# Perceiver block on one core: the last pair's loop is ordered anew, with the expert stage's preparation moved into and ahead of it

## The chip, the cores and the metric

One core of a Trainium2 chip. The metric is the device time of one execution in microseconds (us), of which three runs are shown. TensorE does the matmuls, VectorE, ScalarE and GpSimd the elementwise work, SyncE issues the DMAs. All five run their own instruction streams and meet only at semaphores.

## The reference, cut to what matters

```python
x = x + xattn(ctx, layernorm(x), ...)      # 8 batches, 64 latents, 1024 context rows, 16 heads
x = x + mamba(layernorm(x), ...)           # 8 sequences of 64, 512 inner channels, 16 states
x = x + moe(layernorm(x), ...)             # 8 experts, gathered rows, gelu, weighted scatter-add

# mamba, for each of the 16 states n:
#   h = exp(dt * A[:, n]) * h + dt * x * B[:, n]      a scan over the 64 steps
#   y = y + h * C[:, n]
# then y = (y + x * D) * silu(z), and out = y @ W_out
# moe: h = gelu(rows[idx[e]] @ W1[e] + b1[e]); out[idx[e]] += (h @ W2[e] + b2[e]) * w[idx[e], e]
```

## The kernel before, in words

The 512 latent rows are four tiles of 128, each a pair of batches. Attention takes most of the time. The state scans of pairs 0 to 2 (48 units of one state each) run beside it. For one unit, GpSimd makes the drive (`open_unit`, line 630: dtx times a row of B), ScalarE the decays (line 1423), VectorE the scan (line 974), and GpSimd multiplies with a row of C (`times_c`, line 752); in the last units TensorE adds the products into a PSUM bank with an identity matmul (`sum_unit`, line 1967).

When attention ends, five units of pair 2 are left over (`left`), and pair 3, the last, has not begun: its rows exist only now. From here the kernel goes through these steps:

- The last pair's normalisation, input projection, convolution and time steps. VectorE writes the time steps `dts_l` (line 1194) and `dtx_l` (line 1197), between them the scans of left-overs 0 to 2 and the picks, the 0/1 matrices with which rows are gathered (`first_pick`, line 1033).
- The last pair's loop over 16 states. GpSimd makes drive n (line 777), with four drive buffers. ScalarE writes decays n into PSUM (line 1558). VectorE scans (line 1208) and multiplies with C (`read_open`, line 1218). TensorE adds the product into a bank (`sum_states`, line 2019). GpSimd does left-overs 3 and 4 ahead of drives 0 and 2, VectorE scans them in states 0 and 1, TensorE sums them in states 1 and 2. Pair 2 is gated by VectorE in state 6 (line 1230) and multiplied with W_out in state 8 (line 1808), and its rows are added and their statistics taken in state 11.
- Side jobs in the loop. TensorE turns one pick for each of the experts (line 2024), the coefficients (line 2039) and two products with b2 (line 2048), ScalarE evicts each from the one bank JB (lines 1540, 1543, 1546). Slot weights (line 2062, 4 matmuls for an expert) follow in states 12 to 15, two experts in each. Two of the gather matmuls (line 2054) stand in state 14 and two behind the loop.
- Behind the loop, GpSimd scales each tile's rows (`f_nat`, line 803), ScalarE rounds them (`f_hi`, line 1595), GpSimd subtracts (`f_lo`, line 806). TensorE gathers rows for the experts with 2 matmuls for each of 4 tiles, 2 groups of experts and 2 halves of the channels: 32 in all. The last tile's parts come from VectorE (lines 1250, 1253) and ScalarE.
- ScalarE evicts four banks of gathered rows (line 1577), loads the Gelu table (line 1582) and the experts follow: first products (line 2147), Gelu (line 1587), second products (line 2157), weighting (line 1266), scatter (line 2134).

Each engine's order is written out by hand, and a wait holds up all that is behind it on its engine. Reads of a work buffer wait for its sum (`v_acc`), reads of a product buffer for `sum_states` two states earlier (`m_acc`), and decays n for scan n - 2 (`m_scan`). The rows of B for states 4 to 15 are loaded (`b_all`, line 523) behind the load for left-over 4, which waits for the sum of left-over 0.

## Time and profile before

| | us |
|---|---|
| median of 3 runs | 768.75 |
| lowest, highest | 768.65, 770.01 |
| the profiled execution's own time | 769.03 |
| its span, first to last instruction | 767.3 |

The span is that of the profiled execution; 1.73 us lie around it. Below, PE is TensorE's matmuls, PEld its weight loads, DVE VectorE, ACT ScalarE, POOL GpSimd, SPq the DMA queue. A line of a timeline is one instruction or a run of equal ones (x2 and so on): its start and duration in us, and in brackets the idle time before it with the instruction that ended it. A duration holds the time for which the instruction was held up once it had begun. Consecutive instructions of an engine overlap by some hundredths of a microsecond. The loop goes from VectorE's first scan of line 1208 to the last product of line 1218.

### The profile page before, as it was taken

To read this page: it belongs to the slowest core of one execution; us is meant where nothing else is said; L and a number is where in the kernel's file an instruction comes from. 1 tells how busy PE (TensorE), PEld (TensorE's weight loads), DVE (VectorE), ACT (ScalarE), POOL (GpSimd) and SP (SyncE) were. 2 spreads that over 40 slices of the span, in tenths; PEclk is the share of its full clock that TensorE was granted. 3 is DMA by queue.
4 is the path that set the end of the run, shared out by engine and by line. 5 is a ranking of instruction groups with operands and counts; after the bars stand their busy time and mean duration, and the time that the engine had idled before them with its cause. 6 is when DMAs were issued, how large, how long until landed. Compare 5 with 4: busy or idle time off the path is not lost.

```text
span 767.3 us, 14591 instructions
## 1 busy us (share of the span) xinstructions
PE 735.2 (96%) x5539; PEld 681.3 (89%) x5539; DVE 493.9 (64%) x1061; ACT 432.5 (56%) x1135; POOL 399.7 (52%) x355
## 2 busy tenths in 40 slices
PE   8999999999999999999999999999999886999995
PEld 8889999999998999999989999999999663578885
DVE  7574574556574667858777778686798886840102
ACT  2546456546355766566578666666656553734331
POOL 6515315302610389658838986587397978730000
PEclk9999999999999999999999999999999995999999
DMA  8742100011001200310211022000100107703800
GB/s 308 243 138 60 63 25 2 1 62 25 2 5 59 53 16 1 95 34 16 65 32 34 15 68 55 15 15 1 33 15 21 28 22 234 254 1 129 285 26 30
DMA packets 51418, 49.62 MB, mean 65 GB/s; under 512 B 19524, under 2 KB 46352, under 8 KB 50320
## 3 DMA queue, kind: packets, MB, share of 16 engines
q1 hardware_dynamic: 51344, 48.64, 20.9%
q8 instruction: 46, 0.75, 0.4%
q14 instruction: 28, 0.23, 0.1%
HBM read 44.10 MB, written 4.52 MB: 63 GB/s over the span
## 4 chain that ended last, share of the span: by engine, by line
PE 69%; POOL 14%; issue 8%; DVE 5%; ACT 3%; DMA 1%; POOLq 0%; DVEq 0%
PE psum L1701 18%; PE psum L1736 17%; PE psum L1717 5%; PE psum L2157 4%; PE psum L2147 4%; POOL work L630 3%; PE psum L1670 3%; POOL work L637 2%; POOL y_sum L643 2%; PE psum L1767 2%; PE psum L1677 2%; PE psum L1795 2%; POOL drive L777 1%; PE psum L1611 1%; PE psum L1777 1%
## 5 line engine op out<-in xcount | busy, mean ns | idle before, releaser
L1347 ACT ACTIVATE pt_hi<-psum 128x512 fp32r<-128x512 f32 (+1 forms) x192 | 87.2, 489 | 179.9 <-PE psum L1717 122.0
L1736 PE MATMUL psum<-kvn_hi,pt_hi 128*128 128x256 f32 x512 | 150.1, 293 | 0.0
L1736 PE MATMUL psum<-kvn_hi,pt_lo 128*128 128x256 f32 x512 | 144.3, 282 | 0.0
L1736 PE MATMUL psum<-kvn_lo,pt_hi 128*128 128x256 f32 x512 | 144.2, 282 | 0.0
L1043 DVE TENSOR_REDUCE rowmax<-psum 128x1 f32<-128x728 f32 x64 | 58.6, 915 | 79.2 <-PE psum L1701 79.2
L1736 PEld LDWEIGHTS psum<-kvn_lo,pt_hi 128*128 128x128 f32 x512 | 97.4, 190 | 0.2
L1736 PEld LDWEIGHTS psum<-kvn_hi,pt_hi 128*128 128x128 f32 x512 | 97.1, 190 | 0.2
L1736 PEld LDWEIGHTS psum<-kvn_hi,pt_lo 128*128 128x128 f32 x512 | 97.1, 190 | 0.0
L1701 PE MATMUL psum<-kvt_hi,qk_hi 128*128 128x364 f32 (+1 forms) x384 | 90.5, 344 | 0.0
L896 DVE TENSOR_TENSOR pt_lo<-psum,pt_hi 128x512 fp32r<-128x512 f32 x128 | 82.0, 682 | 8.2 <-ACT pt_hi L1347 8.2
L637 POOL TENSOR_TENSOR work<-work,bc 128x512 f32<-128x512 f32 x40 | 54.3, 1357 | 58.6 <-DVE work L974 58.6
L1701 PE MATMUL psum<-kvt_hi,qk_lo 128*128 128x364 f32 (+1 forms) x384 | 84.5, 328 | 0.0
L1701 PE MATMUL psum<-kvt_lo,qk_hi 128*128 128x364 f32 (+1 forms) x384 | 84.5, 329 | 0.0
L974 DVE TENSOR_TENSOR_SCAN work<-dec,work 128x512 f32<-128x512 f32 x48 | 73.6, 1536 | 6.4 <-POOL work L630 6.1
L575 POOL TENSOR_SCALAR cvar<-cmv 128x8 f32<-128x8 f32 x8 | 1.9, 232 | 131.5 <-DVE cmv L835 131.1
L630 POOL TENSOR_TENSOR work<-dtx,bc 128x512 f32<-128x512 f32 x48 | 65.2, 1361 | 8.4 <-DMA bc<-dbc_keep 6.6
L1717 PE MATMUL psum<-ident,prob 128*128 128x128 f32 x512 | 66.5, 273 | 1.4 <-DVE pt_hi L893 0.8
L1701 PEld LDWEIGHTS psum<-kvt_lo,qk_hi 128*128 128x128 f32 x384 | 66.6, 188 | 0.0
L1701 PEld LDWEIGHTS psum<-kvt_hi,qk_lo 128*128 128x128 f32 x384 | 66.5, 188 | 0.0
L1701 PEld LDWEIGHTS psum<-kvt_hi,qk_hi 128*128 128x128 f32 x384 | 63.2, 189 | 2.2 <-issue 0.4
L1423 ACT ACTIVATE dec<-dts,a_neg 128x126 f32<-128x126 f32 x192 | 60.7, 394 | 5.9 <-DVE work L974 5.3
L1467 ACT ACTIVATE prob<-psum,nbias 128x728 f32<-128x728 f32 x64 | 55.7, 870 | 13.4 <-DVE nbias L1045 11.1
(251 smaller groups left out, 1576.5 us busy)
## 6 DMA issues: line engine op xcount, KB each, us to landing
w<-in_L_ffn_W_dram SPq DMA_DIRECT2D x16, 1024.0 KB, 8.2
ctx_nat<-in_ctx_dram SPq DMA_DIRECT2D x8, 1024.0 KB, 5.1
bc<-dbc_keep SPq DMA_DIRECT2D x48, 128.0 KB, 4.5
q_cur<-q_keep SPq DMA_DIRECT2D x14, 128.0 KB, 3.0
q_keep<-q_t SPq DMA_DIRECT2D x1, 1536.0 KB, 6.0
wq_sb<-in_L_xattn_Wq_dram SPq DMA_DIRECT2D x1, 1024.0 KB, 10.6
wk_nat<-in_L_xattn_Wkv_dram SPq DMA_DIRECT2D x1, 1024.0 KB, 12.7
wv<-in_L_xattn_Wkv_dram SPq DMA_DIRECT2D x1, 1024.0 KB, 14.7
```

The costliest lines, as they stand in the source:

```text
L630: pool.tensor_tensor(work[u % WORKS][:], dtx[:], bc[u % ROWS][:, 0:1, :].to_broadcast((P, DT, P)), ALU.mult).then_inc(v_drv, 1)
L637: link(pool.tensor_tensor(work[u % WORKS][:], work[u % WORKS][:], bc[u % ROWS][:, 1:2, :].to_broadcast((P, DT, P)), ALU.mult))
L896: dve.tensor_tensor(pt_lo[u][:, t0:t1, :], where.rearrange("p (t m) -> p t m", m=P), pt_hi[u][:, t0:t1, :].bitcast(F32), ALU.subtract).the ...
L974: dve.tensor_tensor_scan(work[u % WORKS][:].rearrange(flat), dec[u % 2][:].rearrange(flat), work[u % WORKS][:].rearrange(flat), 0.0, ALU.m ...
L1043: dve.tensor_reduce(rowmax[slot][:, hp, 0:1], LG_A, XY, ALU.max)
L1347: act.activation(pt_hi[u][:, t0:t1, :], where[:, 0:(t1 - t0) * P].rearrange("p (t m) -> p t m", m=P), ACT.Copy)\
L1423: last = act.activation(seqs(dec[u % 2][:])[:, d, :, 1:], seqs(dts[:])[:, d, :, 1:], ACT.Exp, scale=a_neg[:, d, n:n + 1])
L1467: act.activation(prob[hp % 2][:, 0:2 * CUT].rearrange("p (a n) -> p a n", n=CUT), LG_A, ACT.Exp, bias=nbias[slot][:, hp:hp + 1], scale=SCA ...
L1701: last = pe.matmul(psum[:, n, 0:x1_ - x0], w, x_[slot][:, k, x0:x1_], start=first, stop=final)
L1717: last = pe.transpose(TP[n][:, j * P:(j + 1) * P], prob[hp % 2][:, (4 * n + j) * P:(4 * n + j + 1) * P], ident[:])
L1736: pe.matmul(PV, w[u][:, j, :], x_[slot][:, j, :], start=(j == 0 and w is pt_hi and x_ is kvn_hi), stop=False)
L2147: last = pe.matmul(psum[:, f % 4, 0:P], w1[i][:, k, f * P:(f + 1) * P], xg_t[:, k, RING * q + i, :], start=(k == 0), stop=(k == CK - 1))
```

## The change

- GpSimd: behind the last attention left-overs it sets `fhalf`, takes the scales of tiles 0 and 1 in one go and makes all three parts of tile 0, then left-over 1's drive, tile 1's parts, left-over 2's drive. Drives 0 and 1 come ahead of left-over 1's product with C, and the rest of left-overs 1 to 4 is spread between drives 1 and 9. Tile 2's parts and tile 3's scale come behind drive 15.
- VectorE: left-overs 3 and 4 are scanned in states 2 and 4, the gate of pair 2 is in state 9, its addition and statistics in state 12, and the sum of the slot weights in state 10. Behind the loop it makes `f_hi` of the last tile itself, and evicts the second half of each gathered group.
- TensorE: left-overs 2, 3 and 4 are summed in states 1, 5 and 7, W_out of pair 2 is in state 9, the slot weights of one expert in each of the states 1 to 8, and eight gather matmuls (two tiles) in states 12 and 13. The second group gathers into banks 4 and 7.
- ScalarE: it no longer makes `f_hi`, loads the Gelu table ahead of the gathers' evictions, and evicts two banks of gathered rows instead of four.

The diff, cut to its core:

```diff
-        f_nat = [d[:].rearrange("p d m -> p (d m)")[:, h * C:(h + 1) * C] for d in dec for h in range(2)]
+        f_nat = [dec[0][:].rearrange("p d m -> p (d m)")[:, h * C:(h + 1) * C] for h in range(2)]
...
+        f_first = sb(open_, "f_first", [P, 2, C])
+        f_nat = [f_first[:, h, :] for h in range(2)] + f_nat
+        coef_slot = sb(open_, "coef_slot", [P, E])
...
-        GB = (0, 6)
+        GB = ((0, 1), (4, 7))
...
+        SUM_AT = {1: 2, 5: 3, 7: 4}
...
-            for u in left[1:3]:
-                open_unit(u)
+            link(pool.memset(fhalf[:], -0.5))
+
+            def row_scale(t0, t1):
+
+                pool.wait_ge(f_stat, t1)
+                link(pool.tensor_scalar(fvar[:, t0:t1], fmv[:, t0:t1, 1], 1.0, EPS, ALU.mult, ALU.add))
+                link(pool.tensor_tensor(frstd[:, t0:t1], fvar[:, t0:t1], fhalf[:, t0:t1], ALU.pow))
+
+            def row_parts(t):
+
+                pool.tensor_scalar(f_nat[t], x1[:, t, :], fmv[:, t, 0:1], frstd[:, t:t + 1], ALU.subtract,
+                                   ALU.mult).then_inc(f_ln, 1)
+                pool.wait_ge(f_ln, t + 1)
+                pool.tensor_scalar(f_hi[:, t, :], f_nat[t], 1.0, 0.0, ALU.mult, ALU.add).then_inc(f_hi_done, 1)
+                pool.wait_ge(f_hi_done, t + 1)
+                pool.tensor_tensor(f_lo[:, t, :], f_nat[t], f_hi[:, t, :].bitcast(F32), ALU.subtract)\
+                    .then_inc(f_lo_done, 1)
+
+            row_scale(0, 2)
+            row_parts(0)
+            open_unit(left[1])
+            row_parts(1)
+            open_unit(left[2])
...
-            times_c(left[1])
-            open_unit(left[3])
-            times_c(left[2])
-            open_unit(left[4])
             pool.wait_ge(v_dtx, INLINE + 1)
             pool.wait_ge(m_b, 2)
-            for n in range(2):
+            drive_open(0)
+            drive_open(1)
+            times_c(left[1])
+            drive_open(2)
+            open_unit(left[3])
+            drive_open(3)
+            times_c(left[2])
+            pool.wait_ge(ld_ball, 48)
+            drive_open(4)
+            open_unit(left[4])
+            drive_open(5)
+            drive_open(6)
+            times_c(left[3])
+            drive_open(7)
+            drive_open(8)
+            times_c(left[4])
+            for n in range(9, NS):
                 drive_open(n)
-            times_c(left[3])
-            for n in range(2, 4):
-                drive_open(n)
-            times_c(left[4])
-            pool.wait_ge(ld_ball, 48)
-            for n in range(4, NS):
-                drive_open(n)
-
...
+            row_scale(INLINE - 1, INLINE)
+            row_parts(INLINE - 1)
+            row_scale(INLINE, TT)
+            pool.sem_inc(f_rs, 1)
...
-                if n < 2:
-                    scan_unit(left[3 + n])
-                if n == NS - 10:
+                if n == NS - 7:
                     dve.wait_ge(v_acc, NS * INLINE)
                     dve.wait_ge(v_zc, INLINE)
                     gate = zs[(INLINE - 1) % 2]
                     dve.tensor_tensor(gate[:], gate[:], psum[:, WB, :].rearrange("p (d m) -> p d m", m=P), ALU.mult)\
                         .then_inc(v_y, 1)
-                if n == NS - 5:
+                if n == NS - 4:
                     mixed(INLINE - 1, psum[:, WB, 0:C])
                     out_stats(INLINE - 1)
                 if n >= 1:
                     read_open(n - 1)
+                if n in (2, 4):
+                    scan_unit(left[2 + n // 2])
+                if n == NS - 6:
+                    dve.wait_ge(f_cs, 1)
+                    dve.tensor_reduce(coef_slot[:], psum[:, 4, 0:2 * E].rearrange("p (e h) -> p e h", h=2), X, ALU.add)\
+                        .then_inc(f_cse, 1)
...
+            dve.tensor_scalar(f_hi[:, INLINE, :], x1[:, INLINE, :], fmv[:, INLINE, 0:1], frstd[:, INLINE:TT],
+                              ALU.subtract, ALU.mult).then_inc(f_hi_done, 1)
...
+                if isinstance(r, int):
+                    for g in range(EG):
+                        dve.wait_ge(f_gat, CK * (g + 1))
+                        dve.tensor_copy(xg_t[:, 1, g * RING:(g + 1) * RING, :],
+                                        psum[:, GB[g][1], :].rearrange("p (e s) -> p e s", s=P)).then_inc(f_gatd, 1)
...
-                    for k in range(CK):
+                    for k in range(1 if isinstance(r, int) else CK):
                         act.wait_ge(f_gat, CK * EG * r + CK * g + k + 1)
                         act.activation(xg_t[:, k, g * RING:(g + 1) * RING, :],
-                                       psum[:, GB[g] + k, :].rearrange("p (e s) -> p e s", s=P), ACT.Copy)\
+                                       psum[:, GB[g][k], :].rearrange("p (e s) -> p e s", s=P), ACT.Copy)\
                             .then_inc(f_gate, 1)
                 for q in range(EG):
...
+            act.activation(warm_out[:], a_neg[:, 0, 0:1], ACT.Gelu_apprx_tanh)
             longest = longest_list(act)
-            for t in range(TT):
-                act.wait_ge(f_ln, t + 1)
-                act.activation(f_hi[:, t, :], f_nat[t], ACT.Copy).then_inc(f_hi_done, 1)
...
             sum_unit(left[0])
+            spread_out(1)
             sum_unit(left[1])
-            spread_out(1)
-            sum_unit(left[2])
...
-                if n in (1, 2):
-                    sum_unit(left[2 + n])
                 sum_states(n)
-                if n == NS - 8:
+                if n in SUM_AT:
+                    sum_unit(left[SUM_AT[n]])
+                if n == NS - 7:
                     pe.wait_ge(v_y, INLINE)
                     w_out(zs[(INLINE - 1) % 2], psum[:, WB, 0:C]).then_inc(v_yo, 1)
                 if 1 <= n < E + 4:
                     side_job(n - 1)
-                weigh = n - E - 4
-                if weigh == 0:
+                if n == 1:
                     pe.wait_ge(f_hl, 1)
                     pe.wait_ge(m_b, 2)
-                if 0 <= weigh < E // 2:
-                    slot_weight(2 * weigh)
-                    last = slot_weight(2 * weigh + 1)
-                    if weigh == E // 2 - 1:
+                if 1 <= n <= E:
+                    last = slot_weight(n - 1)
+                    if n == E:
                         last.then_inc(f_cs, 1)
-                if n == NS - 2:
-                    pe.wait_ge(f_b2e, CK)
-                    pe.wait_ge(f_lo_done, 1)
-                    gather(1, 1, 0)
-            pe.wait_ge(f_b2e, CK)
-            pe.wait_ge(f_lo_done, 1)
-            gather(1, 0, 0)
+                t = n - E - 4
+                if t == 0:
+                    pe.wait_ge(f_b2e, CK + 1)
+                    pe.wait_ge(f_cse, 1)
+                if t in (0, 1):
+                    pe.wait_ge(f_lo_done, t + 1)
+                    for k in range(CK):
+                        gather(1, k, t)
...
-            for t in range(1, INLINE):
-                pe.wait_ge(f_lo_done, t + 1)
-                for k in range(CK):
-                    gather(1, k, t)
+            pe.wait_ge(f_lo_done, INLINE)
+            for k in range(CK):
+                gather(1, k, INLINE - 1)
```

## Rows read from the trace of the kernel before

**Rows 1.** The page: the span of the profiled execution.

```profile
span 767.3 us, 14591 instructions
```

**Rows 2.** Windows view: stretch; busy us (instructions) by engine; TensorE clock; DMA share, GB/s.

```profile
core 0: us, PE busy (x) PEld busy (x) DVE busy (x) ACT busy (x) POOL busy (x), PEclk, DMA share, GB/s
634.00:653.00 19.00, 13.70 (x27) 6.29 (x28) 12.92 (x13) 7.15 (x24) 16.50 (x13) 0.55 0.77 251
```

**Rows 3.** Chain of waits in order of time: start us, us, what, around the loop's end and the first expert.

```profile
678.56 0.79 PE psum L2062 x8
...
682.12 1.73 PE psum L1808 x8
683.85 5.14 PE psum L2054 x22
...
689.01 2.07 ACT xg_t L1577 x4
...
691.09 1.28 ACT L1582
...
695.41 3.72 PE psum L2157 x16
699.13 3.57 PE psum L2147 x32
```

**Rows 4.** Timeline of GpSimd: start us, us, line, operation, out<-in, count [idle before].

```profile
618.26 3.41 POOL L752 TENSOR_TENSOR work<-work,bc 128x512 f32<-128x512 f32 x2
622.98 1.27 POOL L630 TENSOR_TENSOR work<-dtx,bc 128x512 f32<-128x512 f32 x1 [1.30 <-PE psum L1967]
627.32 1.31 POOL L630 TENSOR_TENSOR work<-dtx,bc 128x512 f32<-128x512 f32 x1 [3.07 <-DMA bc<-dbc_keep]
...
639.19 2.48 POOL L777 TENSOR_TENSOR drive<-dtx_l,b_all 128x512 f32<-128x512 f32 x2
```

**Rows 5.** Timeline of GpSimd near the loop's end.

```profile
668.43 0.56 POOL L800 TENSOR_TENSOR frstd<-fvar,fhalf 128x1 f32<-128x1 f32 x1
669.21 1.23 POOL L803 TENSOR_SCALAR dec<-x,fmv,frstd 128x256 f32<-128x256 f32 x1 [0.22 <-POOL frstd L800]
675.96 0.73 POOL L806 TENSOR_TENSOR f_lo<-dec,f_hi 128x256 fp32r<-128x256 f32 x1 [5.52 <-ACT f_hi L1595]
```

**Rows 6.** Timeline of GpSimd near the kernel's start.

```profile
10.04 1.05 POOL L568 TENSOR_SCALAR x_hi<-x_lat 128x1024 fp32r<-128x1024 f32 x1 [1.97 <-DVE x_lat L854]
```

**Rows 7.** Timeline of VectorE ahead of the last pair's loop.

```profile
618.41 2.21 DVE L974 TENSOR_TENSOR_SCAN work<-dec,work 128x512 f32<-128x512 f32 x1 [0.89 <-POOL work L630]
...
633.27 2.29 DVE L1033 TENSOR_TENSOR pick<-iota_f,slot_of 128x1024 fp32r<-128x1024 f32 x1
640.56 1.22 DVE L1208 TENSOR_TENSOR_SCAN state<-psum,drive 128x512 f32<-128x512 f32 x1 [5.00 <-POOL drive L777]
```

**Rows 8.** Timeline of VectorE at the loop's end and after it.

```profile
676.71 1.26 DVE L1218 TENSOR_TENSOR read<-state,psum 128x512 f32<-128x512 f32 x2
...
683.89 0.42 DVE L1244 TENSOR_TENSOR x<-x,psum 128x256 f32<-128x256 f32 x1 [2.39 <-PE psum L1808]
...
686.00 0.41 DVE L1250 TENSOR_SCALAR dec<-x,fmv,frstd 128x256 f32<-128x256 f32 x1 [1.01 <-POOLq L801]
686.89 0.43 DVE L1253 TENSOR_TENSOR f_lo<-dec,f_hi 128x256 fp32r<-128x256 f32 x1 [0.49 <-ACT f_hi L1595]
```

**Rows 9.** Timeline of TensorE in and after the last pair's loop.

```profile
647.09 2.08 PE L2019 MATMUL psum<-read,ident 128*128 128x512 f32 x2 [4.76 <-DVE read L1218]
...
652.11 1.02 PE L1967 MATMUL psum<-work,ident 128*128 128x512 f32 x2
...
658.67 1.13 PE L2019 MATMUL psum<-read,ident 128*128 128x512 f32 x2 [0.32 <-DVE read L1218]
...
668.66 0.60 PE L2039 MATMUL psum<-ident,coef 128*8 128x128 f32 x4
...
679.75 1.02 PE L2019 MATMUL psum<-read,ident 128*128 128x512 f32 x2
```

**Rows 10.** Timeline of ScalarE in the loop.

```profile
669.66 0.57 ACT L1543 ACTIVATE coef_t<-psum 8x512 f32<-8x512 f32 x1
```

58 lines of the change are left out of this document (27 added, 31 removed).

## The prediction, made before the result was known

> **What bounds the kernel now.** I first read the page and the chain of waits for the whole span [rows 1], then timelines of each engine from 616 us on, since every edit lies there. The expert stage starts in earnest when TensorE begins the first expert's second products at 695.41 us; behind it TensorE hardly pauses [rows 3]. So the question is when that instruction starts. Three stretches lead to it.
>
> Ahead of the loop GpSimd is the late one. VectorE is done with its last pick at 635.56 and sits idle for 5.00 us until drive 0 is there; the loop's first scan starts at 640.56 [rows 7]. GpSimd was idle itself for 1.30 and 3.07 us earlier [rows 4]. In the loop the last product ends at 676.71 + 1.26 = 677.97, 37.4 us after the first scan [rows 8]. Behind the loop TensorE is the late one: it adds the last state only at 679.75 [rows 9], since slot weights and gathers stand in its queue, and then works off 22 gather matmuls in 5.14 us (0.234 each), after which ScalarE evicts for 2.07 us and loads a table for 1.28 [rows 3]. From the last product to 695.41 it takes 17.4 us.
>
> One mechanism matters throughout. A VectorE instruction whose two inputs lie in SBUF, and a GpSimd instruction, do not overlap. The scan at 618.41 took 2.21 us, the pick at 633.27 took 2.29, each held until GpSimd's instruction was over; the loop's scan, with one input in PSUM, took 1.22 beside GpSimd [rows 7]. GpSimd in turn took 3.41 us for two products that need 2.5 [rows 4].
>
> **Stretch 1, ahead of the loop.** GpSimd is free at 618.26 + 3.41 = 621.67 [rows 4]. From there it now has, up to the end of drive 0:
> - small operations for the scales: a memset and an addition (my estimate 0.4 with gaps) and a power of 0.56 [rows 5], a little more for two columns: 1.2 us together.
> - two times the rows' parts. `f_nat` 1.23, `f_lo` 0.73 [rows 5]. `f_hi` on GpSimd is not in this stretch. Its nearest row is a rounding with the same two constants, 1024 wide, 1.05 us [rows 6]; by width a quarter of it, with some fixed cost 0.4. The upper bound is `f_nat`'s 1.23, the same width but with two scalars read from memory. I take 0.4, as the operation is the same. With gaps, 2 x 2.6 = 5.2 us.
> - two left-over drives, one product with C, drive 0 at 1.24 [rows 4], `y_skip` (0.9) and the two small coefficient operations (0.5): 6.4 us.
>
> That is 12.8 us of its own work. Its two idle times are gone, so all of VectorE's two-input work now falls beside a busy GpSimd and holds it: two scans, two picks, `dts_l`, `dtx_l` and the latents' scaling, by the free durations about 1.0 + 1.0 + 1.0 + 1.1 + 0.65 + 0.7 + 0.3 = 5.75 us. Sum: 621.67 + 12.8 + 5.75 = 640.2. The first scan starts at 640.25, 0.3 us earlier. The four operations that leave this stretch (two products, two drives) are paid back by the rows' parts. With `f_hi` at 1.23 it would be 641.9.
>
> The Trainium skill, "GPSIMD Engine Reference", Engine selection, calls one-input work on GpSimd roughly line-rate and sends elementwise work to VectorE. By line rate the rounding of 256 columns would be an estimated 0.21 us and the sum 0.4 us less for two of them; by its advice the move is a loss. The trace has `f_nat` at 1.23 us on GpSimd [rows 5] and at 0.41 on VectorE [rows 8], which speaks for the advice and against line rate.
>
> **Stretch 2, the loop.** Up to state 5 GpSimd sets the pace: from drive 1 to drive 4 come six operations of 1.24, held by the third pick (1.1) and the scan of left-over 3 (1.1), so scan 4 can start 11.0 us into the loop. Then two scans and two products more (1.13 and 0.6 by their pitch), the scan of left-over 4 (1.1) and a wait of 0.7 for GpSimd ahead of it bring product 5 to 18.0 us, 658.3. Before, TensorE began to add state 5 at 658.67 [rows 9]: the same place, with both left-overs scanned in both.
>
> From there TensorE is the late one. Before, it went from state 5's sum at 658.67 to the coefficients' transpose at 668.66, that is 10.0 us for five sums of states, four turned picks, one spreading of C and W_out of pair 2 [rows 9], of which some 0.7 us were waits (0.32 ahead of the first). The change adds to the same stretch two sums of left-overs at 1.05 (1.02 by the row, and a gap [rows 9]) and four slot weights at 0.79 / 2 = 0.40 [rows 3]: 10.0 - 0.7 + 2.1 + 1.6 = 13.0. The transpose starts at 658.35 + 13.0 = 671.35. VectorE waits for it twice: at the gate of state 9 (for left-over 4's sum, 1.2 us) and at the new sum of the slot weights in state 10, behind which scan 11 is queued (1.1 us). ScalarE evicts the coefficients at 671.9 instead of 669.66 [rows 10], and behind that eviction stand decays 13, 14 and 15, each behind a side job. From the eviction to the last product it was 677.97 - 669.66 = 8.3 us and is 8.1 now. The last product ends at 680.0, **2.1 us later** than before.
>
> The loads of B are issued some 5 us later, as they hang on the sum of left-over 0; drive 4 is asked for at about 650, the loads should land at about 648. The experts' weights come 5 us later as well, and the first of them is not read before 686. Both I cost at nothing; if the first cover is gone, scan 4 waits by as much.
>
> **Stretch 3, behind the loop.** Counted from the last product: TensorE has only states 14 and 15 queued, so the last sum is done at +1.5 (before at +2.8, 679.75 + 1.02), VectorE's gate takes 0.7, W_out starts at +2.3 instead of +4.0, the row addition ends at +4.7 instead of +6.34 (683.89 + 0.42 [rows 8]). The last tile's `f_lo` ended 3.0 us after that addition (686.89 + 0.43 [rows 8]) and will again: one more VectorE operation of 0.4 in place of ScalarE's rounding: +7.7. TensorE has 4 + 12 gathers at 0.234 up to there, from +3.9: +7.65, in balance. So the last eight gathers start at +7.7 instead of at 688.34, that is +10.4: 2.7 us gained. From their start to xg ready it stays 1.9 us, as VectorE's copy (0.66 for 512 columns out of PSUM, half of 1.26 [rows 8]) is no faster than ScalarE's second (2.07 / 4 = 0.52 [rows 3]). But the table is loaded by then and ScalarE has two evictions less, so the first expert runs at TensorE's pace: 3.73 us for its first products, last Gelu 0.4: second products at +7.7 + 1.9 + 4.2 = +13.8 instead of +17.4. Gained: **3.6 us**. The experts' stage is unchanged.
>
> **Sum.** -0.3 is contained in the loop's end: +2.1 - 3.6 = -1.5 us. The profiled execution took 769.03 (span 767.3), 0.28 above the median of 768.75; its span would be 765.8 and its time 767.5, and against the median 767.2. A measurement of this kernel can tell about 0.2% (1.5 us) from no change, so this stands on that line.
>
> **The rivals.**
> - *The loop does not get longer (764.9).* If the sums and slot weights fit into TensorE's waits, the loop takes 37.7 us or less and -3.6 and -0.3 stand. For it: TensorE waited for products at 647.09 [rows 9], and is idle early in the loop. Against it: those waits are ahead of state 5, the added work is behind it.
> - *Drive 0 comes early (763.5).* Where GpSimd's `f_nat` and `f_hi` do not hold VectorE's scans and picks and dts_l is not late, the loop starts up to 3.5 us earlier. The rows show the hold for products alone. The Trainium skill, "SBUF — State Buffer", SBUF: two separate sides, says that any GpSimd operation holds the shared ports for its whole length; by that rule this rival falls.
> - *The gain is given back (768.7).* Each slot weight costs more than 0.40 alone, between other kinds of work, or `f_hi` costs 1.23 twice: the loop ends 1.5 us later still, and the time is the same.
> - *TensorE stays at the lower clock (772, slower).* In 634 to 653 us the granted clock was 0.55, near the lower level of 1.2 GHz; one sum of a state took 2.08 us at 647.09 and 1.02 for a pair of the same matmuls at 652.11 [rows 2, 9]. It rose after TensorE had worked without a pause from 647.09. The new order spreads TensorE's work there, with waits for products with C between. If the clock rises only at state 5, some 10 us of work up to there takes 20, the products wait, and the loop is about 5 us longer. It decides from the point where the clock is below 0.8 over the loop's first 16 us.
> - *The change does less than it says (767.9 to 768.7)*: the last tile's `f_lo` and not the gathers ends last behind the loop. This only moves the gain by a few tenths.
>
> **How the numbers follow.** My forecast (766.2 to 768.2) has 0.42, half of it below the line of 0.2%. The unchanged loop has 0.18, the early drive 0.08, the gain given back 0.12, the clock 0.10, and 0.10 are for a loop that is longer by 4 to 5 us by GpSimd's costs or late loads (769.5 to 771). Faster: 0.22 + 0.18 + 0.08 = 0.48. Same: 0.20 + 0.12 = 0.32. Slower: 0.20. The range runs from the early drive, 763.5, to 770.6, which leaves out the clock and a part of the last.
>
> **What would show it.** In the changed profile: first scan at 640.2 (early drive: 637); granted clock over the loop's first 16 us above 0.6; TensorE without waits between states 5 and 9 and the coefficients' transpose 13 us after state 5's sum; scan 11 waiting about 1 us for the slot weights; last product at 680.0; the first Gelu without a table load ahead and 13.8 us from the last product to the second products of the first expert. I am wrong in stretch 2 if ScalarE evicts the coefficients before 670, and in stretch 1 if GpSimd is idle ahead of drive 0.

## The result and the profile after

Five runs of the changed kernel have a median of 764.91 us (764.06 to 766.17), beside 769.04 us (768.65 to 770.01) for five of the kernel before. The ratio is 0.9948, with a 95% interval of 0.9937 to 0.9960: faster by half a per cent, more than the 0.2% that can be told from no change. The prediction said 767.2. 764.91 is inside its whole range (763.5 to 770.6), but below the core of it (766.2 to 768.2): the direction was right, and the gain of 4.1 us is more than twice the 1.55 forecast (768.75 to 767.2).

| us | before | predicted | after |
|---|---|---|---|
| latents scaled (`xn`) to the loop's first scan | 24.28 | 24.0 | 22.14 |
| the loop, first scan to last product | 37.41 | 39.8 | 39.88 |
| last product to the first second products | 17.44 | 13.8 | 14.37 |
| span | 767.3 | 765.8 | 764.0 |
| the profiled execution's time | 769.03 | 767.5 | 765.70 |

The span is 3.3 us shorter: 2.14 us less in the first stretch, 2.47 more in the loop, 3.07 less behind it. The other 0.56 (0.33 ahead of `xn`, 0.23 behind the second products) lie in stages that the change does not touch; single executions of the kernel before differ by more than that (768.65 to 770.01).

**Ahead of the loop.** GpSimd's timeline of the changed kernel has no idle time from its products on, where [rows 4] had 1.30 and 3.07 us.

```profile
621.76 0.72 POOL L771 TENSOR_TENSOR frstd<-fvar,fhalf 128x2 f32<-128x2 f32 x1
622.58 1.23 POOL L775 TENSOR_SCALAR f_first<-x,fmv,frstd 128x256 f32<-128x256 f32 x1
623.89 0.42 POOL L778 TENSOR_SCALAR f_hi<-f_first 128x256 fp32r<-128x256 f32 x1
624.39 0.73 POOL L780 TENSOR_TENSOR f_lo<-f_first,f_hi 128x256 fp32r<-128x256 f32 x1
625.08 1.32 POOL L633 TENSOR_TENSOR work<-dtx,bc 128x512 f32<-128x512 f32 x1
626.39 2.20 POOL L775 TENSOR_SCALAR f_first<-x,fmv,frstd 128x256 f32<-128x256 f32 x1
...
635.74 3.46 POOL L801 TENSOR_TENSOR drive<-dtx_l,b_all 128x512 f32<-128x512 f32 x2
```

VectorE's timeline beside it, with its two waits for TensorE in the loop and the ones at its end:

```profile
626.50 1.23 DVE L995 TENSOR_TENSOR_SCAN work<-dec,work 128x512 f32<-128x512 f32 x1 [1.23 <-POOL work L633]
627.64 1.35 DVE L1054 TENSOR_TENSOR pick<-iota_f,slot_of 128x1024 fp32r<-128x1024 f32 x1
...
638.09 1.22 DVE L1229 TENSOR_TENSOR_SCAN state<-psum,drive 128x512 f32<-128x512 f32 x1 [1.23 <-POOL drive L801]
...
661.87 0.69 DVE L1249 TENSOR_TENSOR zs<-zs,psum 128x512 f32<-128x512 f32 x1 [0.93 <-PE psum L2000]
...
665.56 0.17 DVE L1260 TENSOR_REDUCE coef_slot<-psum 128x8 f32<-128x16 f32 x1 [0.69 <-PE psum L2094]
...
677.28 0.69 DVE L1239 TENSOR_TENSOR read<-state,psum 128x512 f32<-128x512 f32 x1 [1.02 <-PE psum L2051]
```

The first scan waits 1.23 us for drive 0, not 5.00 [rows 7]. The wait of 1.02 ahead of the last product was on nobody's list.

**In the loop.** The windows view (as rows 2): the loop's first 16 us, the stretch between state 5's sum and the coefficients' transpose, and the loop's end.

```profile
638.09:654.09 16.00, 13.33 (x49) 7.34 (x49) 15.32 (x15) 8.68 (x27) 16.00 (x11) 0.77 0.75 263
655.52:668.05 12.53, 12.53 (x64) 8.54 (x64) 10.23 (x13) 8.43 (x25) 10.95 (x10) 1.00 1.04 364
668.00:672.50 4.50, 4.50 (x14) 1.45 (x11) 4.09 (x8) 3.43 (x10) 2.70 (x6) 1.00 0.04 13
672.50:676.00 3.50, 3.50 (x7) 2.04 (x7) 3.20 (x4) 3.20 (x7) 0.67 (x1) 0.54 0.00 0
```

TensorE is busy 12.53 of 12.53 us in the second row: it is the late engine, as predicted. In the last row its granted clock falls to 0.54, with no pause ahead of it (TensorE's timeline has no idle time between 647.29 and 679.8 us). TensorE's timeline there:

```profile
655.52 1.10 PE L2051 MATMUL psum<-read,ident 128*128 128x512 f32 x2
...
668.05 0.60 PE L2071 MATMUL psum<-ident,coef 128*8 128x128 f32 x4
...
670.50 1.12 PE L2051 MATMUL psum<-read,ident 128*128 128x512 f32 x2
671.55 1.12 PE L2080 MATMUL psum<-coef_t,b_sb 8*128 8x512 f32 x2
672.60 1.95 PE L2051 MATMUL psum<-read,ident 128*128 128x512 f32 x2
```

The sum of state 12 takes 1.95 us where the one before it took 1.12, and the four gathers behind it take 1.71 where the next four take 0.94. So state 13's sum comes late, and VectorE waits 1.02 us for it ahead of its last product.

**Behind the loop.** The chain of waits (start, us, what), which was [rows 3]:

```profile
678.08 1.73 PE psum L2051 x4
...
680.58 1.99 PE psum L1841 x8
682.57 5.62 PE psum L2086 x24
688.19 3.70 PE psum L2182 x32
...
691.92 0.38 ACT hid L1622
```

Evictions (2.07) and table load (1.28) are gone from the chain; the first expert's matmuls follow the gathers at once. ScalarE loads the table at 674.45.

**The profiled execution and the median.** The profiled execution is 0.8 us above the median. Its mean granted clock over the span is 0.985, as in the run of 766.17; the three runs of 764.06 to 764.91 have 0.987. The experiments below put the fall of the clock at 1.5 us (1.1 in the loop and 0.4 behind it), near the distance between these two groups (1.4). That the faster three had no fall is not shown: only the profiled execution has a trace, and the mean clock does not tell the fall by itself, as later traces without it have means from 0.984 to 0.990.

### The profile page after: what moved, and what is told of

It is laid out like the page before. It is cut to its first block, busy times and chain, and to the rows that moved or that the text cites. A ratio compares the mean times of both kernels' runs of the same rounds, so it can differ in the third digit from the quotient of the medians.

```text
span 764.0 us, 14587 instructions
## 1 busy us (share of the span) xinstructions
PE 733.6 (96%) x5539; PEld 681.2 (89%) x5539; DVE 498.0 (65%) x1064; ACT 430.7 (56%) x1128; POOL 399.8 (52%) x356
## 4 chain that ended last, share of the span: by engine, by line
PE 71%; POOL 15%; issue 7%; DVE 4%; ACT 2%; POOLq 0%; DVEq 0%
PE psum L1734 18%; PE psum L1769 17%; PE psum L1750 5%; PE psum L2182 4%; PE psum L2194 4%; POOL work L633 3%; PE psum L1703 3%; POOL work L640 2%; POOL y_sum L646 2%; PE psum L2051 2%; PE psum L1800 2%; PE psum L1710 2%; PE psum L1810 1%; PE psum L1684 1%; PE psum L1644 1%
```

## The experiments

All are made from the changed kernel unless it says otherwise. "First scan" is counted from `xn`, "tail" from the last product to the first expert's second products. At the end stands a table of all.

### The changed kernel again

No edit. 

> The changed kernel once more, beside the next ones on the same chip. In its first profile the granted TensorE clock fell to 0.50 from 673 to 676 us, at the end of the loop, and in none of the four experiments since. Theory: the fall belongs to that one execution, not to the order: here the clock stays at 1.00 from 650 to 690 us, the loop takes 38.8 us (as with the late table and with two tensors) instead of 39.9, and the second products start 14.0 us behind the last product instead of 14.4. Rival: this order brings the fall, since TensorE's stream in states 10 to 12 is all long matmuls: it is there again.

Measured: first scan 22.10, loop 39.88, tail 14.36, ratio 0.9947 (0.9933 to 0.9960). Everything repeats to 0.05 us, the fall of the clock too (0.58 in 672 to 676 us). My theory, an accident of one execution, is refuted. Whether the fall is in every execution the runs do not show: four of these five have a mean clock of 0.987 and no trace.

### The Gelu table behind the evictions

```diff
-                    if not isinstance(r, int):
-                        act.activation(warm_out[:], a_neg[:, 0, 0:1], ACT.Gelu_apprx_tanh)
+                    act.activation(warm_out[:], a_neg[:, 0, 0:1], ACT.Gelu_apprx_tanh)
...
-            act.activation(warm_out[:], a_neg[:, 0, 0:1], ACT.Gelu_apprx_tanh)
             longest = longest_list(act)
```

> The changed kernel with one part undone: ScalarE loads the Gelu table again behind the evictions of the gathered rows, and before each group of experts. My theory: the early table is worth what it takes out of ScalarE's stream ahead of the first Gelu, 1.28 + 0.20 us, less what TensorE's own pace hides (the 8 first products come every 0.47 us, a Gelu every 0.36): the first expert's second products start 0.6 to 1.1 us later than in the changed kernel, counted from the last eight gathers (7.2 us there with second products at 6.2), and the span grows by the same. Rival: the early load is hidden anyway since TensorE sets the pace there: second products at 6.2 us, span the same within 0.3 us.

Measured: first scan 22.11, loop 38.78, tail 14.34; ratio 0.9947 (0.9931 to 0.9964). ScalarE's timeline:

```profile
686.61 1.28 ACT L1616 ACT_TABLE_LOAD   x1
687.90 0.20 ACT L1616 ACTIVATE warm_out<-a_neg 128x1 f32<-128x1 f32 x1
688.01 2.86 ACT L1621 ACTIVATE hid<-psum,b_t 128x128 f32<-128x128 f32 x8
```

The Gelus start late but take 2.86 us instead of 3.49, since their inputs are all waiting. The kernels without a fall of the clock have a tail of 13.98, so the early table is worth 0.36 us, about a quarter of the load and less than the 0.6 to 1.1 of my theory. And here, with the same order on TensorE, the clock did not fall: the loop took 38.8.

### ScalarE evicts all four banks

```diff
-                        dve.tensor_copy(xg_t[:, 1, g * RING:(g + 1) * RING, :],
-                                        psum[:, GB[g][1], :].rearrange("p (e s) -> p e s", s=P)).then_inc(f_gatd, 1)
...
-                    for k in range(1 if isinstance(r, int) else CK):
+                    for k in range(CK):
```

with TensorE's waits on those evictions adapted. 

> The changed kernel, but ScalarE evicts all four banks of gathered rows as before the change; the Gelu table stays ahead of them. Theory (the table was what cost, the second evictor buys almost nothing, as ScalarE's Gelus catch up): the last eviction ends 0.2 us later, the first Gelu starts 0.3 to 0.4 later, eight Gelus then take 3.1 to 3.2 us instead of 3.49 since they no longer wait for TensorE, and the second products come 14.0 to 14.1 us after the last product (14.4 if the clock falls near the loop's end); time within 0.1 us of the changed kernel. Rival (the evictions are on the path): second products 0.5 us later or more, 14.5 (14.9 with the fall of the clock), and 0.5 us more time.

Measured: loop 38.77, tail 13.91; 764.87 us, ratio 0.9949 (0.9933 to 0.9965). ScalarE's timeline:

```profile
685.11 2.07 ACT L1609 ACTIVATE xg_t<-psum 128x512 f32<-128x512 f32 x4 [9.39 <-PE psum L2084]
687.03 3.46 ACT L1620 ACTIVATE hid<-psum,b_t 128x128 f32<-128x128 f32 x8
```

The first Gelu starts 10.40 us after the last product, no later than with two evictors (10.43 in the last experiment below), where I had expected 0.3 to 0.4 later. The time and the tail came as the theory said, but not by Gelus that catch up: they take 3.46 us, as before. The second evictor is worth nothing once the table is early: VectorE's copy takes 0.69 us where ScalarE's takes 0.52.

### Slot weights back in the last states

Two experts' slot weights in each of states 12 to 15, their sum behind the loop, two gathers in state 14 and two behind the loop, as before the change. The second group again gathers into banks 6 and 7.

```diff
+                weigh = n - E - 4
...
-                if 1 <= n <= E:
-                    last = slot_weight(n - 1)
...
+                if 0 <= weigh < E // 2:
+                    slot_weight(2 * weigh)
+                    last = slot_weight(2 * weigh + 1)
```

> The changed kernel with TensorE's slot weights and gathers put back as before: slot weights two experts a state in states 12 to 15, one gather of two matmuls in state 14, one behind the loop, tiles 1 and 2 behind W_out, and the sum of the slot weights behind the loop. Everything else as changed. My theory: the loop is held up by TensorE's queue in states 5 to 9, so without slot weights there the loop gets shorter, from 39.9 us to about 38, while the way from the last product to the second products of the first expert grows from 14.4 to about 16.5: the sum is 0 to 1 us slower than the changed kernel. Rival: moving them is the main gain: the loop stays at 39.9 us, the tail grows by 2 to 3 us and all of it is lost.

Measured: loop 37.65, tail 16.55, ratio 0.9960 (0.9946 to 0.9974), clock 1.00 to the loop's end. Of the changed kernel's loop without a fall, 38.8, the loop gets back 1.1 us, and the tail loses 2.6. The coefficients' transpose comes 1.1 earlier (28.84 after the first scan), less than the 1.6 to which I had priced the four slot weights behind state 5's sum: one takes 0.34 us in the chain where I had 0.40, which makes 1.36. Loop and tail are 54.2 us here and 52.8 in the changed kernel without a fall, so this part of the change is worth about 1.4 us at full clock (0.8 by the medians).

### W_out of pair 2 behind state 12

W_out moves from state 9 to state 12, the addition of pair 2 and its statistics behind the loop, the gathers one state later.

```diff
-                if n == NS - 7:
-                    pe.wait_ge(v_y, INLINE)
-                    w_out(zs[(INLINE - 1) % 2], psum[:, WB, 0:C]).then_inc(v_yo, 1)
...
+                if n == NS - 4:
+                    pe.wait_ge(v_y, INLINE)
+                    w_out(zs[(INLINE - 1) % 2], psum[:, WB, 0:C]).then_inc(v_yo, 1)
```

> The changed kernel with pair 2's W_out on TensorE in state 12 instead of 9 (behind the side jobs), the addition of its rows and their statistics on VectorE behind the last product (where it waits for TensorE anyway), the sum of the slot weights in state 12 instead of 10, and the two in-loop gathers one state later. My theory: in states 5 to 9 TensorE's queue is what ends last, and ScalarE's side jobs and decays hang on it, so taking 1.73 us out ahead of the coefficients' transpose brings it from 30.0 to 28.2 us after the first scan, takes away VectorE's wait of 0.7 us for the slot weights, and shortens the loop from 38.8 to about 37.3; behind the loop some 0.3 us are lost where tile 2's rows come late. Sum 0.8 to 1.5 us faster than the changed kernel. Rival: the loop's end is bound by VectorE and by the chain of side jobs behind the coefficients, which does not start earlier because ScalarE is late itself: loop within 0.3 us of the changed kernel's, and the tail 0.3 to 1 us longer: same or slower.

Measured: transpose 28.23, loop 37.37, tail 15.31, ratio 0.9940 (0.9927 to 0.9954). The transpose is 1.73 us earlier, W_out's length, and the loop follows by 1.4. Nearly all of it is paid back in the tail (1.33 us, where I had expected 0.3), where TensorE still has W_out and the gathers in front of the last sum:

```profile
673.21 1.02 PE L2050 MATMUL psum<-read,ident 128*128 128x512 f32 x2
...
676.80 1.02 PE L2050 MATMUL psum<-read,ident 128*128 128x512 f32 x2
678.60 1.99 PE L1840 MATMUL psum<-wout,dtx_l 128*128 128x256 f32 x8 [0.78 <-DVE dtx_l L1264]
```

So from 655 us on it is TensorE's total that counts here, not where W_out stands. A shorter loop is no gain by itself; loop and tail together are 52.7 here and 52.8 in the changed kernel without a fall, and my 0.8 to 1.5 us of gain did not come (0.7 by the medians).

### The old order of drives and left-overs

The changed kernel, but GpSimd does left-overs 1 to 4 ahead of and between drives 0 to 4 as before; VectorE scans left-overs 3 and 4 in states 0 and 1, TensorE sums them in states 1 and 2. The rows' parts stay where the change has them.

```diff
+            times_c(left[1])
+            open_unit(left[3])
+            times_c(left[2])
+            open_unit(left[4])
             pool.wait_ge(v_dtx, INLINE + 1)
...
-            drive_open(0)
-            drive_open(1)
-            times_c(left[1])
+            for n in range(2):
+                drive_open(n)
```

(The sum of left-over 2 goes ahead of the loop again, and the gate, W_out and the addition of pair 2 are in states 6, 8 and 11 as before. Slot weights and their sum stay.) 

> The changed kernel with the left-overs' order put back as before on GpSimd (two products and two drives of left-overs ahead of drive 0, then two drives, product, two drives, product), on VectorE (scans of left-overs 3 and 4 in states 0 and 1, gate in state 6, addition in state 11) and on TensorE (sums in state 1 and 2, W_out in state 8). The rows' parts of tiles 0 and 1 stay ahead of the loop, slot weights and gathers stay as changed. My theory: four operations of 1.24 us come back ahead of drive 0, the first scan starts 4 to 6 us later than the 638.1 of the changed kernel, the loop gets shorter by about 3 us (37 instead of 39.9): the span is 1.5 to 3 us longer than the changed kernel's. Rival: the order of drives only shifts where the wait falls, GpSimd's total being the same: loop shorter by as much as it starts later, span the same within 0.5 us.

Measured: first scan 27.55, loop 41.49, tail 13.98, ratio 1.0081 (1.0053 to 1.0108): slower than the kernel before. Its four runs lie at 772.54, 772.64, 776.06 and 776.64 us, with mean clocks of 0.983 in the first two and 0.975 and 0.974 in the others; the trace is of 772.64, and what cost the slower two another 4 us has no trace. VectorE's timeline, TensorE's, and the windows view of two overlapping stretches:

```profile
643.54 1.22 DVE L1224 TENSOR_TENSOR_SCAN state<-psum,drive 128x512 f32<-128x512 f32 x1 [6.64 <-POOL drive L801]
...
673.56 0.17 DVE L1255 TENSOR_REDUCE coef_slot<-psum 128x8 f32<-128x16 f32 x1 [3.17 <-PE psum L2090]
```

```profile
650.07 2.07 PE L2047 MATMUL psum<-read,ident 128*128 128x512 f32 x2 [4.42 <-DVE read L1234]
...
676.55 1.12 PE L2047 MATMUL psum<-read,ident 128*128 128x512 f32 x2 [1.63 <-DVE read L1234]
```

```profile
644.00:648.00 4.00, 1.64 (x3) 0.29 (x1) 4.00 (x4) 1.24 (x4) 1.57 (x2) 0.84 0.98 279
648.00:656.00 8.00, 5.93 (x12) 2.73 (x13) 6.92 (x9) 2.47 (x8) 8.00 (x7) 0.57 1.06 377
```

VectorE had waited 5.00 for it before [rows 7]. Two results. The order of the drives is worth 27.55 - 22.14 = 5.4 us of the first scan, where I had let it pay just for the rows' parts. And the loop, of which my theory had said that it would be about 3 us shorter, is 2.7 longer than the changed kernel's 38.78 without a fall. The clock has a part in it: it was 1.00 between 645.5 and 648.5 us, TensorE waited 4.42 us for the first product, and from 649 to 655 the clock was 0.50. That is near the rival "TensorE stays at the lower clock", in a kernel that was not predicted; it rose and fell back. But it accounts for 0.8 us at most, since the coefficients' transpose comes 30.79 us after the first scan, where it was 29.96. The other 1.9 us lie behind the transpose, at full clock: W_out stands in state 8 here, ahead of the last slot weight, so VectorE waited 3.17 us for the slot weights, and TensorE then 1.63 for the product of state 10.

### The rows' parts behind the drives

```diff
-            row_scale(0, 2)
-            row_parts(0)
             open_unit(left[1])
-            row_parts(1)
             open_unit(left[2])
...
+            row_scale(0, 2)
+            row_parts(0)
+            row_parts(1)
             row_scale(INLINE - 1, INLINE)
             row_parts(INLINE - 1)
```

and the eight gathers of tiles 0 and 1 behind the loop. 

> The changed kernel with the rows' parts of tiles 0 and 1 on GpSimd behind drive 15, where they stood before (the rounding still on GpSimd), and their gathers behind W_out. Drives stay ahead of the left-overs. My theory: GpSimd loses 6.3 us of work ahead of drive 0 but gets back its waits for the sum of a left-over and for a load (1.3 and 3.1 us before), so the first scan starts 1.5 to 2.5 us earlier than the 22.1 us after the normalised rows; the tail grows by 8 gathers of 0.234 us, 1.9 us, and by what GpSimd is late with the third tile's parts, up to 3 us. Sum: 0 to 2 us slower than the changed kernel. Rival: the parts' place costs the start all of its 6 us, and moving them back is a gain: first scan 4 to 6 us earlier, time 1 us faster or more.

Measured: first scan 19.64, loop 38.77, tail 15.83, ratio 0.9937 (0.9922 to 0.9952). GpSimd's timeline:

```profile
622.29 1.27 POOL L633 TENSOR_TENSOR work<-dtx,bc 128x512 f32<-128x512 f32 x1 [1.29 <-PE psum L2000]
626.92 1.26 POOL L633 TENSOR_TENSOR work<-dtx,bc 128x512 f32<-128x512 f32 x1 [3.36 <-DMA bc<-dbc_keep]
...
632.92 3.40 POOL L798 TENSOR_TENSOR drive<-dtx_l,b_all 128x512 f32<-128x512 f32 x2 [0.63 <-DVE dtx_l L1218]
```

GpSimd's old waits are back, and still the loop starts 2.5 us earlier. The rows' parts with their scales, 6.3 us of work, fill waits of 4.7 us and cost 2.5. The tail loses 1.85 us for the eight gathers, 8 x 0.234 = 1.87. So preparing two tiles early buys less than it costs; the changed kernel would be better without it, by 0.6 us at full clock and 1.1 by the medians, where I had expected it to be better with it.

### Tile 1's first part in another form

In the parts of tile 1 alone, GpSimd's scaling with two numbers from memory is replaced by a product of two tensors of the same width. Tile 1's rows are then not those of the reference.

```diff
-                pool.tensor_scalar(f_nat[t], x1[:, t, :], fmv[:, t, 0:1], frstd[:, t:t + 1], ALU.subtract,
-                                   ALU.mult).then_inc(f_ln, 1)
+                if t == 1:
+                    pool.tensor_tensor(f_nat[t], x1[:, t, :], x1[:, t - 1, :], ALU.mult).then_inc(f_ln, 1)
+                else:
+                    pool.tensor_scalar(f_nat[t], x1[:, t, :], fmv[:, t, 0:1], frstd[:, t:t + 1], ALU.subtract,
+                                       ALU.mult).then_inc(f_ln, 1)
```

> The changed kernel with tile 1's scaled rows on GpSimd made by a multiplication of two tensors (x of tile 1 by x of tile 0, 256 columns) instead of the subtraction and multiplication with two scalars from memory, so tile 1's rows for the experts are not the reference's. It meets VectorE's scan of left-over 1, which in the changed kernel took 1.23 us (not held) while the GpSimd instruction took 2.20 instead of 1.23. Theory: the form with two scalars from memory does not hold VectorE in its first part, whoever comes first; a multiplication of two tensors does. Then the scan takes 1.7 to 2.0 us and the multiplication 0.73. Rival: it is a matter of who comes first by some hundredths of a microsecond, not of the form: the scan again takes 1.23 and the multiplication is held to about 1.7.

Measured: first scan 22.24, loop 38.78, tail 13.98. GpSimd's and then VectorE's timeline:

```profile
626.66 0.72 POOL L776 TENSOR_TENSOR f_first<-x 128x256 f32<-128x256 f32 x1
627.47 1.20 POOL L781 TENSOR_SCALAR f_hi<-f_first 128x256 fp32r<-128x256 f32 x1
628.75 1.57 POOL L783 TENSOR_TENSOR f_lo<-f_first,f_hi 128x256 fp32r<-128x256 f32 x1
...
636.21 2.18 POOL L804 TENSOR_TENSOR drive<-dtx_l,b_all 128x512 f32<-128x512 f32 x1 [0.63 <-DVE dtx_l L1221]
```

```profile
626.80 1.66 DVE L998 TENSOR_TENSOR_SCAN work<-dec,work 128x512 f32<-128x512 f32 x1 [1.23 <-POOL work L633]
628.39 1.35 DVE L1057 TENSOR_TENSOR pick<-iota_f,slot_of 128x1024 fp32r<-128x1024 f32 x1
```

A two-tensor product holds the scan (1.66 us, and 0.72 for itself); the scaling does not (scan 1.23), but takes 2.20 us itself. GpSimd had started first both times, by 0.14 and 0.11 us, so in these two traces it is the form and not the order of starts that decides which engine is held. The loop's first scan hardly moves (22.24 for 22.14): `f_hi` and `f_lo` are now held (1.20 and 1.57 us), and GpSimd then waits 0.63 us for VectorE's `dtx_l`.

### Tile 1's parts behind left-over 2's drive

```diff
             open_unit(left[1])
-            row_parts(1)
             open_unit(left[2])
+            row_parts(1)
```

> The changed kernel with tile 1's parts on GpSimd behind the drive of left-over 2 instead of ahead of it. My theory: GpSimd's total of own work and of time held by VectorE sets drive 0, and neither changes: first scan at 22.1 us after the normalised rows, within 0.3. Rival: what sets it is VectorE's chain (scan of left-over 2 ahead of the time steps), which gets the drive 2.5 us earlier: first scan 0.5 to 1 us earlier.

Measured: first scan 23.24, loop 39.99, tail 13.98, 766.43 us in its one run. The first scan was expected where it was and came 1.1 us later:

```profile
626.69 1.68 POOL L633 TENSOR_TENSOR work<-dtx,bc 128x512 f32<-128x512 f32 x1 [0.71 <-DMA bc<-dbc_keep]
628.37 2.18 POOL L775 TENSOR_SCALAR f_first<-x,fmv,frstd 128x256 f32<-128x256 f32 x1
630.63 1.44 POOL L778 TENSOR_SCALAR f_hi<-f_first 128x256 fp32r<-128x256 f32 x1
```

GpSimd waits 0.71 us for left-over 2's row of B, and three operations in a row are held (1.68, 2.18 and 1.44 for 1.27, 1.23 and 0.42). The same work in another order meets other VectorE instructions. The loop is 1.2 us longer too, without a fall of the clock:

```profile
649.14 1.26 POOL L801 TENSOR_TENSOR drive<-dtx_l,b_all 128x512 f32<-128x512 f32 x1 [1.19 <-PE psum L2000]
```

This is drive 4, ahead of which GpSimd's program waits for the loads of B; they were issued at 643.1 to 644.0 us, 2.2 later than in the changed kernel, and took up to 5.1 us to land. The matmul that the profile names ends at the same moment, but drive 4 does not wait for it. VectorE's scan 4 then waited 1.90 us.

### Tile 0's parts in the wait, tile 1's behind the drives

Tile 0's parts move between the drives of left-overs 1 and 2 (where GpSimd waits for a load in the kernel of rows' parts last), tile 1's behind drive 15; the gathers come one state later.

```diff
-            row_parts(0)
             open_unit(left[1])
-            row_parts(1)
+            row_parts(0)
             open_unit(left[2])
...
+            row_parts(1)
             row_scale(INLINE - 1, INLINE)
```

> The changed kernel with the scales taken where GpSimd waits for a left-over's sum (1.3 us with the rows late), tile 0's parts behind left-over 1's drive, where it waits for a load (3.4 us), tile 1's parts behind drive 15, and the two gathers in the loop in states 13 and 14 instead of 12 and 13. My theory: what the parts cost ahead of drive 0 is GpSimd's own time beyond its waits; 1.2 us of scales and 2.5 us of tile 0's parts fit into them, so the first scan comes 19.6 to 20.3 us after the normalised rows as with all rows late (22.1 in the changed kernel), while the tail keeps its eight gathers in the loop: 14.0 us and not 15.8. Against the changed kernel 2 to 3 us faster, against the rows-late one 1 to 1.8. Rival: every part in this stretch is paid, because it also holds VectorE's scan of left-over 1 and pick: first scan at 21 us or later, and the time that of the rows-late kernel.

Measured: first scan 20.12, loop 39.08, tail 15.34, ratio 0.9937 (0.9924 to 0.9951). One tile's parts (with the scales of both) cost 0.48 us there instead of half of 2.5. But the tail is not the 14.0 that I had expected: the clock fell again (0.61 over 670 to 674 us), and tile 1's gathers now stand ahead of the last sum. So this kernel is not faster than the one with both tiles' parts behind the drives (763.77).

The same with left-over 2's sum in state 2 instead of 1: `SUM_AT = {2: 2, 5: 3, 7: 4}`. 

> The same, and left-over 2 is summed by TensorE in state 2 instead of 1, behind which TensorE stood 0.65 us for GpSimd's product in the changed kernel; the chain of waits ran over TensorE alone from there to the loop's end. My theory: the loop is TensorE's work from state 1 on, so the wait is given back in full: loop 38.1 instead of 38.8, time 0.5 us less than the kernel with only tile 0 moved. Rival: the sum then waits in state 2 or later states wait for ScalarE's side jobs, which have not become earlier: loop 38.8, same time.

Measured: first scan 20.12, loop 38.77, tail 14.91, ratio 0.9933 (0.9919 to 0.9946), no fall in its trace. My theory had the loop at 38.1. It stays at the 38.77 of the other traces without a fall, as the rival said: TensorE's wait of 0.59 us for left-over 2's product is gone, and one of 1.02 for a product of VectorE stands in its place.

### Tile 1's gathers in TensorE's wait for the gate

On top of the last one:

```diff
-                if t in (0, 1):
-                    pe.wait_ge(f_lo_done, t + 1)
+                if t == 0:
+                    pe.wait_ge(f_lo_done, 1)
                     for k in range(CK):
-                        gather(1, k, t)
+                        gather(1, k, 0)
+            pe.wait_ge(f_lo_done, 2)
+            for k in range(CK):
+                gather(1, k, 1)
             pe.wait_ge(v_y, INLINE + 1)
```

> Tile 0's parts stand between the drives of left-overs 1 and 2, tile 1's parts behind drive 15, left-over 2 is summed in state 2, all as in tile0_sum2. New: tile 1's four gathers stand behind state 15's sum, ahead of W_out, instead of ahead of state 15's sum. Theory (TensorE sets the end of the tail, and it waits 0.78 us there for VectorE's gate): the last sum starts 0.9 us earlier (675.6 instead of 676.46), the gathers (0.94 us) fill the wait for the gate, W_out starts 0.7 us earlier, and the first expert's second products come 14.2 us after the last product instead of 14.9. First scan 20.1 us after the latents are scaled, loop 38.8, span 761.1, time 762.9. Rival (the tail is set by VectorE's chain of gate, addition and parts, not by TensorE's order): the gathers delay W_out by as much as they leave, the second products stay at 14.9, and the time stays at 763.6. If the granted clock falls to 0.5 near 673 us, add 1.1 to the loop and 0.4 to the tail.

Measured: first scan 20.12, loop 38.77, tail 13.98, 762.61 us (761.91 to 763.35), ratio 0.9916 (0.9902 to 0.9929). TensorE's timeline:

```profile
673.94 1.98 PE L2051 MATMUL psum<-read,ident 128*128 128x512 f32 x4
675.36 0.80 PE L2086 MATMUL psum<-pick,f_hi 128*128 128x512 f32 x1
...
676.71 1.99 PE L1841 MATMUL psum<-wout,dtx_l 128*128 128x256 f32 x8
```

There is no idle time ahead of W_out any more, and the tail is 0.93 us shorter, a little more than expected. This version beats both kernels: 2.3 us under the changed one by the medians.

### All runs beside each other

| | first scan | loop | tail | clock falls near the loop's end | median | ratio |
|---|---|---|---|---|---|---|
| before | 24.28 | 37.41 | 17.44 | no | 769.04 | |
| after | 22.14 | 39.88 | 14.37 | yes | 764.91 | 0.9948 |
| again | 22.10 | 39.88 | 14.36 | yes | 764.95 | 0.9947 |
| late table | 22.11 | 38.78 | 14.34 | no | 764.67 | 0.9947 |
| one evictor | 22.13 | 38.77 | 13.91 | no | 764.87 | 0.9949 |
| slot weights late | 22.10 | 37.65 | 16.55 | no | 765.74 | 0.9960 |
| W_out late | 22.14 | 37.37 | 15.31 | no | 764.25 | 0.9940 |
| old order | 27.55 | 41.49 | 13.98 | no | 774.35 | 1.0081 |
| parts behind drives | 19.64 | 38.77 | 15.83 | no | 763.77 | 0.9937 |
| other form | 22.24 | 38.78 | 13.98 | no | 765.03 (one) | |
| parts swapped | 23.24 | 39.99 | 13.98 | no | 766.43 (one) | |
| tile 0 in the wait | 20.12 | 39.08 | 15.34 | yes | 764.33 | 0.9937 |
| with sum in state 2 | 20.12 | 38.77 | 14.91 | no | 763.57 | 0.9933 |
| gathers in the wait | 20.12 | 38.77 | 13.98 | no | 762.61 | 0.9916 |

## Why the prediction was right, and where it was not

It was right that the kernel gets faster, and that it does so behind the loop at the loop's cost. The size was 2.3 us off by the medians, so that less than half of the gain was forecast. In the profiled executions the miss is 1.8 us: the first scan was 2.16 us earlier than the 640.25 forecast (0.33 of it lies ahead of `xn`), the tail 0.57 longer than forecast.

**Stretch 1: the step that failed is the term for the held instructions, 5.75 us.** GpSimd's own work came out as priced: scales 1.3 us from memset to power (1.2), parts of tile 0 2.5 (2.6), `f_hi` 0.42 (0.4, where 1.23 was the other bound). From the memset at 621.29 to the end of drive 0 at 638.1 it took 16.8 us, so with 12.8 of its own 4.0 were holds. The largest part of the difference lies in the scan and the pick beside tile 1's `f_nat`: 2.0 us of holds in the sum, 0.97 for `f_nat` and 0.17 for `f_hi` in the trace, since VectorE's scan (1.23) ran through it. The holds beside the next scan, `dts_l`, `dtx_l` and the second pick were 0.1 to 0.2 shorter each than priced. The latents' scaling cost GpSimd nothing either: `f_lo` beside it took its free 0.73 (0.3 of hold in the sum). The rival "drive 0 comes early" needed exactly this, that `f_nat` does not hold the scans. It came true for that one operation, and the first scan came 2.1 us earlier, of that rival's 3.5 (its 763.5, the lower end of my range, should have been 767.2 - 3.5 = 763.7). The Trainium skill, "SBUF — State Buffer", SBUF: two separate sides, says that whichever of the two starts first gets the ports for the whole instruction and the other fully blocks; `f_nat` had started first (626.39, the scan at 626.50) and was the one that took longer, so the trace does not agree for this form. For products of tensors it agrees: the scan that began 0.14 us behind one was held to 1.66.

My sentence that the operations leaving the stretch are "paid back by the rows' parts" is what two experiments put numbers on: the order is worth 4.6 us without parts (24.28 to 19.64) and 5.4 with them; the parts cost 2.5 in the new order and 3.3 in the old one. Behind the drives the same work stands beside GpSimd's idle time and costs TensorE's gathers, 1.85. The Trainium skill, "GPSIMD Engine Reference", Engine selection, would leave such work to VectorE; the durations agree (1.23 us on GpSimd, 0.41 on VectorE), but the experiments show that where the work stands decides, 0.48 us for one tile in a wait.

**Stretch 2** is right in its sum, 39.88 for 39.8, by two errors that cancel. State 5's sum came 17.4 us into the loop (18.1 forecast), the transpose 12.53 us behind it (13.0 forecast; slot weights 0.34 each, not 0.40), VectorE's waits were 0.93 and 0.69 (1.2 and 1.1). With the 8.65 us that I had behind the transpose that makes 38.6; the traces of the same order without the fall show 38.8. The fall of the clock added 1.1. The rival "the loop does not get longer" gave 764.9, the number that came, but its mechanism is refuted: the loop is 1.4 us longer even at full clock. That its time came out is luck: the early drive 0 gave it.

**Stretch 3**: 13.98 at full clock, 13.8 forecast. Of 3.5 us gained at full clock (17.44 to 13.98), the slot weights and gathers that left it make 2.6, the table 0.36, the second evictor nothing; the last 0.5 was not taken apart and stays open. I had given table and evictors 0.9 together; the Gelus take back most of it, since they go through waiting inputs at 0.36 us each and through TensorE's pace at 0.44. `f_lo` of the last tile ended at +8.03 (686.00) for +7.7 in an execution with the fall; TensorE's gathers were in balance with it, as forecast.

**The clock.** Early in the loop it is 0.77 over the first 16 us. That is above the 0.6 of my signs and below the 0.8 that I had set for the slower rival, two points that did not fit each other. The loop did not suffer: state 5's sum came earlier than forecast, TensorE was 13.33 us busy of 16 (before 11.23 by the same view), and the clock was at 1.00 from 645.5 us on. The point of 0.8 was set too high. The fall to the lower level at 672.8 us, behind a stretch in which TensorE was busy for 4.50 of 4.50 us, was not among my cases. In the changed kernel it costs 1.5 us, with tile 0 in the wait 0.3 in the loop and 0.4 behind it. What decides whether it comes is open: three traces show it near the loop's end, and three with the same order on TensorE (late table, other form, one evictor) do not, two of them with the same first scan after `xn` to 0.05 us. One thing differs in the traces: in the three with the fall the clock had risen 7.4, 7.2 and 7.5 us into the loop, in the other three 8.6, 5.6 and 8.6. No run shows that this is the cause. I had a theory of one unlucky execution; the repetition spoke against it.

**The loads of B and of the experts' weights** came later and cost nothing, as costed: GpSimd did not wait ahead of drive 4, and no expert's matmul in the chain for a weight. But the margin for B was small. Drive 4 was asked for at 647.2, not at 650, and by the landing times (5.1 us at most, the last load issued at 641.7) the rows were there at about 646.8, an estimate. With tile 1's parts swapped the loads came 2.2 us later, and GpSimd waited 1.19 us.

## What to carry to other kernels

When one engine is late ahead of a loop, order its queue by who waits for each result, and put preparation where the trace shows that it waits for a load or for another engine, not simply early: the parts of one tile cost 0.48 us inside a wait, and those of two tiles cost 2.5 ahead of it. When an engine is busy without a pause through two stretches, a shorter first stretch is no gain; only work taken away, or put in a wait (here the 0.78 us for the gate), is. Check, too, which result the moved work stands in front of: with the old order, W_out ahead of one slot weight cost more than the low clock did. And price a load or an eviction that is taken off the path together with how fast its followers then catch up.

## What the runs showed of the hardware that I had not expected

- GpSimd's scaling of 128x256 with two numbers from memory takes 1.23 us free and 2.20 beside VectorE's two-input scan and pick, which took 1.23 and 1.35. The product of two tensors takes 0.72 and held the scan to 1.66.
- The same operation with two constants takes 0.40 to 0.42 us on GpSimd, as much as `f_hi` on VectorE (0.41).
- TensorE's granted clock fell to its lower level for 3.4 us in the middle of uninterrupted work (0.54 over 672.5 to 676.0 us, 1.00 and fully busy before). A state's sum then took 1.95 us, four gathers 1.71 instead of 0.94.
- With the old order the clock rose at 645.3 us and fell back at 648.7, in a wait of TensorE of 4.42 us that had begun at 645.65; it was 0.50 from 649 to 655 us.
- The early Gelu table (1.28 us) is worth 0.36.
